# Moving the attention output projection into the first round of experts, with fewer buffers behind it

## The chip, the cores and the metric

The kernel runs on the eight cores of one Trainium2 chip. Each core computes one of the eight sequences of the batch by itself, with its own copy of all weights; no core sends anything to another. The metric is device time: the microseconds of the slowest core for one execution. In the text TensorE is PE in the profile's rows, VectorE is DVE, ScalarE is ACT, GpSimd is POOL, and SyncE is SP. PEld is TensorE's load of the stationary operand.

## The reference, cut to what matters

The layer is a parallel block: the layer norm of x feeds an attention and a mixture of 32 experts, and both are added to x. Per core x is 2048 tokens of 2048 features.

```python
xn = layernorm(x)
# attention, 32 heads of 64, "stick-breaking" weights
z   = q @ k.T / 8 ;  lom = where(mask, -softplus(z), 0)
att = where(mask, exp(log_sigmoid(z) + reverse_cumsum(lom) - lom), 0)
attn = concat_heads(att @ v) @ Wo.T
# experts: all low rank (R = 128), inner width I = 1408
rg, ru = xn @ Rg.T, xn @ Ru.T
for e in range(32):
    g  = silu(rg @ Ug[e].T @ Cg[e].T) ;  u = ru @ Uu[e].T @ Cu[e].T
    y += w[:, e, None] * ((g * u) @ Rd.T @ Ud[e].T @ Cd[e].T)
# one shared expert of the same form with inner width 2816, weight 1
out = x + attn + y + shared
```

w is the top-4 softmax gate, with zeros for the experts that are not chosen. The kernel computes every expert for every token, as the reference does.

## The kernel before, in words

A small recorder (class Sched, L41 to L159) puts each instruction on its engine's list in the order in which the Python code calls it, and works out the semaphore waits from named resources. Each engine executes its own list strictly in that order. Three properties of the recorder matter here:

- A DMA that writes a resource waits for the last writer of that resource, and a whole tile is one resource. So several DMAs that fill parts of one tile run one after the other, each after the landing of the one before.
- A wait for a DMA means a wait for the count that its slot (its semaphore) has reached at the time of recording, and so for every DMA recorded on that slot up to then.
- A read or a write of a part of a tile counts as one of the whole tile.

The stages are: layer norm and gates; attention, head pair by head pair, into the tile oF (64 KB in each partition); the output projection (L715 to L745); and the experts (L749 to L957). In passing, during attention, GpSimd casts the weights of the experts and Wo into scratch tensors in DRAM (scr_cgu, scr_cd, scr_u3, scr_wo).

The projection has four feature blocks ft of 512 columns and 16 token blocks tc. For each ft, 16 DMAs of 128 KB fill one of two wo tiles. For each tc, TensorE adds up 16 matmuls (the weights of Wo against oF) in bank 0 or 1, SyncE loads the piece of x (xp), VectorE adds the two (L740), and SyncE stores the sum.

The experts run over four token blocks tt of 512 tokens. Within a tt, two lanes take turns on all engines. Lane 0 takes the even experts and then the shared one and owns PSUM banks 0 to 3; lane 1 takes the odd experts and owns banks 4 to 7. A turn of a lane is one piece of a generator, here called a slot. An expert (L789) has 15 slots: one with the loads for expert e+2, one head (three matmuls and three copies in a row, L799 to L813), eleven steps over c, one tail (L834 to L844), and one empty one in which the generator ends. A step over c is: two matmuls into banks b1 and b2 (L816, L819), SiLU on ScalarE (L822), the matmul of the previous c by Rd (L826), and a product on VectorE (L830). The shared expert (L847) has 25 slots, 22 of them steps. One turn of both lanes is called a round.

After its units each tt has two sweeps ("half", L916). A sweep holds 256 tokens in eight PSUM banks, and adds up 33 steps of eight matmuls, one step for each expert (L932) and one for the shared expert (L939). The Cd tile of an expert (512 KB) is loaded from DRAM for each sweep, into one of three cd buffers, two steps ahead. At the end VectorE copies four banks into yst0 and four into yst1, and for each an accumulating DMA (L954, slot yacc) adds them to the output in DRAM.

Of the kernel before, what the change touches and what calls it, by code (L numbers as in the profile page):

```python
# [204 lines left out]
def build_program(upto="full", taps=()):  # L205
# [504 lines left out]
    s3 = ExitStack()  # L710
    t_wo2 = [sb(f"wo{i}", [128, NHC * QT], BF16, s3) for i in range(2)]
    t_xp = [sb(f"xp{i}", [128, QT], F32, s3) for i in range(2)]
    t_outp = [sb(f"op{i}", [128, QT], F32, s3) for i in range(3)]
# [1 line left out]
    for ft in range(4):  # L715
        wsl = ft % 2
        t_wo = t_wo2[wsl]
        rwo = res(f"wo{wsl}")
        for hc in range(NHC):
            Sc.dma("POOL", f"lwo{wsl}", lambda s, hc=hc, ft=ft, t_wo=t_wo: s.dma_start(  # L720
                t_wo[:, hc * QT:(hc + 1) * QT],
                d_wo[hc * 128:(hc + 1) * 128, ft * QT:(ft + 1) * QT]),
                reads=[res(f"scr_wo{hc}")], writes=[rwo])
        for tc in range(16):
            bk = tc % 2
            for hc in range(NHC):
                Sc.op("PE", lambda t, hc=hc, tc=tc, ft=ft, bk=bk, t_wo=t_wo: t.matmul(  # L727
                    pbank[bk][:, 0:QT],
                    t_oF[:, hc * S + tc * 128: hc * S + tc * 128 + 128],
                    t_wo[:, hc * QT:(hc + 1) * QT],  # L730
                    start=(hc == 0), stop=True, skip_group_check=(hc != 0)),
                    reads=[roF, rwo], writes=[pr[bk]])
            xs = tc % 2
            rxp = res(f"xp{xs}")
            Sc.dma("SP", f"lxp{xs}", lambda s, tc=tc, ft=ft, xs=xs: s.dma_start(
                t_xp[xs][:], dx[tc * 128:(tc + 1) * 128, ft * QT:(ft + 1) * QT]),
                writes=[rxp])
            osl = tc % 3
            rop = res(f"op{osl}")
            Sc.op("DVE", lambda v, bk=bk, xs=xs, osl=osl: v.tensor_tensor(  # L740
                t_outp[osl][:], pbank[bk][:, 0:QT], t_xp[xs][:], op=ALU.add),
                reads=[pr[bk], rxp], writes=[rop])
            Sc.dma("SP", "sout", lambda s, tc=tc, ft=ft, osl=osl: s.dma_start(
                dout[tc * 128:(tc + 1) * 128, ft * QT:(ft + 1) * QT], t_outp[osl][:]),
                reads=[rop], writes=[OUT_rb[tc]])  # L745
    close_scope(s3)
    close_scope(s_oF)

    s4 = ExitStack()  # L749
    t_rdT = sb("rdT", [128, NIC * 128], BF16, s4)  # L750
    t_su3 = sb("su3", [128, 3 * R], BF16, s4)
    t_scg = sb("scg", [128, SI], BF16, s4)
    t_scu = sb("scu", [128, SI], BF16, s4)
    t_srd = sb("srd", [128, NSC * 128], BF16, s4)
    t_scd = sb("scd", [128, H], BF16, s4)
# [3 lines left out]
    ldc(t_scg[:], dr["sCgT"], "scg", slot="lsh")
    ldc(t_scu[:], dr["sCuT"], "scu", slot="lsh")  # L760
    for c in range(NSC):
        ldc(t_srd[:, c * 128:(c + 1) * 128], dr["sRdT"][c * 128:(c + 1) * 128, :], "srd", slot="lsh")
    ldc(t_scd[:], dr["sCdT"], "scd", slot="lsh")

    t_cgu = [sb(f"cgu{i}", [128, 2 * I], BF16, s4) for i in range(4)]
    t_u3 = [sb(f"u3_{i}", [128, 3 * R], BF16, s4) for i in range(4)]
    t_cd = [sb(f"cd{i}", [128, H], BF16, s4) for i in range(3)]
    t_zg = [sb(f"zg{i}", [128, QT], BF16, s4) for i in range(2)]
    t_zu = [sb(f"zu{i}", [128, QT], BF16, s4) for i in range(2)]
    t_g = [sb(f"g{i}", [128, NIC * QT], BF16, s4) for i in range(2)]  # L770
    t_gu = [sb(f"gu{i}", [128, NIC * QT], BF16, s4) for i in range(2)]
    t_wb = [sb(f"wb{i}", [128, QT], BF16, s4) for i in range(2)]
    t_rds = [sb(f"rds{i}", [128, QT], BF16, s4) for i in range(2)]
    t_zd = sb("zd", [128, (E + 1) * QT], BF16, s4)
    t_werow = [sb(f"werow{i}", [1, QT], BF16, s4) for i in range(4)]
    t_yst = [sb(f"yst{i}", [128, H], F32, s4) for i in range(2)]
# [120 lines left out]
    for tt in range(NTT):  # L897
        for e0 in range(4):
            emit_eloads(e0, tt)
        units = [gen_expert(e, tt, e % 2) for e in range(E)]  # L900
        units.append(gen_shared(tt, 0))
# [76 lines left out]
```

How the kernel before makes its waits and increments, by code:

```python
                def body(e, ops=ops):  # L151
                    for waits, fn, inc_key, inc_n in ops:
                        for (s, v) in waits:
                            e.wait_ge(handles[s], v)
                        if fn is not None:
                            inst = fn(e)
                            if inc_n:
                                inst.then_inc(handles[inc_key], inc_n)
```

## Time and profile before

| | value |
|---|---|
| median of 3 runs | 8514.58 us (8486.89 to 8533.01) |
| profiled execution, its own time | 8456.38 us |
| span of its slowest core (core 2), first to last instruction | 8454.8 us |
| spans of the eight cores | 8384.8 to 8454.8 us |
| TensorE busy, and its weight loads | 5396.6 us (64%), 1591.9 us (19%) |
| VectorE, ScalarE, GpSimd busy | 39%, 34%, 10% |
| granted TensorE clock, mean of core 2 | 0.705 |
| attention ends, projection ends, last sweep ends (core 2) | 4922, 5302, 8428 us |

Busy shares are means over stages that have different limits, so they are read by stage. The granted clock is a share of full speed. A busy TensorE in the profile is not TensorE at its peak, since the recorded durations of matmuls overlap: a 512-column matmul lasts 379 ns in the rows and the next can start 216 ns after it at full clock.

### The profile page before, as it was taken

The numbers are of one execution on the slowest core, as the hardware profiler recorded it, in microseconds if no ns is written. First come the engines' busy times: TensorE is split into PE (matmuls) and PEld (weight loads), VectorE is DVE, ScalarE is ACT, GpSimd is POOL, SyncE is SP. The second block draws the span as 40 slices with busy tenths as digits, with TensorE's granted clock in tenths as the row PEclk, the third lists the DMA queues.
The fourth block names the chain that finished last, engine by engine and source line by source line (L and its number), as shares of the span: only waits on it lengthen the run. The fifth ranks groups of instructions, "written<-read, shape, count | busy, mean of one in ns | idle before, by whom it ended". The sixth has DMA issues, their size and how long they took to land.

```text
span 8454.8 us, 81234 instructions; the slowest of 8 cores (8384.8 to 8454.8 us)
## 1 busy us (share of the span) xinstructions
PE 5396.6 (64%) x17259; PEld 1591.9 (19%) x17588; DVE 3256.7 (39%) x5812; ACT 2889.1 (34%) x4306; POOL 854.1 (10%) x1617
## 2 busy tenths in 40 slices
PE   2222556677766777777677657377667757767776
PEld 0011111122211222221122112112211221122212
DVE  7211224344444444444444411266156425514650
ACT  0000234344444444444444510145044314413440
POOL 0001111110001111000110000100100010011001
PEclk9866655666655666665566579688878887787768
...
GB/s 76 12 5 10 61 52 89 67 12 6 6 6 7 8 8 7 6 6 6 7 8 1 1 68 119 67 55 47 152 82 55 78 148 55 55 122 105 52 35 171
DMA packets 222122, 408.82 MB, mean 48 GB/s; under 512 B 141576, under 2 KB 144032, under 8 KB 215760
## 3 DMA queue, kind: packets, MB, share of 16 engines
...
q10 hardware_dynamic: 272, 0.14, 0.0%
...
## 4 chain that ended last, share of the span: by engine, by line
PE 47%; DMA 16%; DVE 13%; ACT 11%; issue 11%; DVEq 1%; ACTq 0%; SPq 0%; POOL 0%; POOLq 0%; another core or an unknown queue 0%
PE pbq L511 7%; PE zp L646 6%; PE zp L640 5%; DMA cd<-scr_cd 5%; ACT att L566 5%; PE pboA L580 4%; PE zp L549 4%; DVE gu L830 3%; DVE lsb L652 3%; DMA xp<-x 3%; PE pboB L580 3%; ACT g L822 2%; PE pbL L819 2%; DMA wv<-WvT 2%; PE zp L819 2%
## 5 line engine op out<-in xcount | busy, mean ns | idle before, releaser
L652 DVE TENSOR_TENSOR lsb<-zp,z 1x512 bf16<-1x512 f32 (+3 forms) x1152 | 668.3, 588 | 1324.5 <-PE zp L646 1308.7
L580 PE MATMUL pboA<-att,vtok 128*64 128x512 bf16 (+2 forms) x640 | 346.9, 542 | 885.5 <-ACT att L566 738.0
L607 ACT ACTIVATE texp<-zp 128x1024 bf16<-128x1024 f32 x448 | 458.8, 1024 | 912.4 <-PE zp L549 737.3
L566 ACT ACTIVATE att<-zp 128x1024 bf16<-128x1024 f32 x448 | 458.4, 1023 | 679.3 <-DVE lsb L652 439.9
L646 PE MATMUL zp<-lsb,ones 1*128 1x512 bf16 (+2 forms) x1152 | 611.2, 531 | 33.4 <-issue 31.2
L640 PE MATMUL zp<-sp,tri 128*128 128x512 bf16 (+3 forms) x1199 | 596.3, 504 | 55.6 <-DVE z L627 49.0
L627 DVE COPY z<-zp 1x512 f32<-1x512 f32 (+3 forms) x1152 | 623.8, 577 | 0.6 <-issue 0.2
L830 DVE TENSOR_TENSOR gu<-g,pbL 128x512 bf16<-128x512 bf16 x704 | 484.3, 688 | 200.2 <-PE pboB L816 79.1
L830 DVE TENSOR_TENSOR gu<-g,zp 128x512 bf16<-128x512 bf16 x704 | 484.3, 688 | 177.3 <-PE zp L816 56.6
L802 ACT ACTIVATE zg<-zp 128x512 bf16<-128x512 f32 x64 | 38.2, 597 | 1413.8 <-PE zp L799 1413.8
L822 ACT ACTIVATE g<-zp 128x512 bf16<-128x512 f32 x704 | 420.5, 597 | 289.9 <-PE zp L816 221.8
L822 ACT ACTIVATE g<-pboB 128x512 bf16<-128x512 f32 x704 | 420.5, 597 | 243.5 <-PE pboB L816 172.6
L610 ACT ACTIVATE sp<-texp 128x1024 bf16<-128x1024 bf16 x448 | 473.1, 1056 | 42.8 <-ACT texp L607 2.3
L932 PE MATMUL zp<-cd,zd 128*128 128x512 bf16 x1004 | 312.1, 402 | 227.6 <-DMA cd<-scr_cd 221.9
L549 PE MATMUL zp<-q,k 64*128 64x512 bf16 (+3 forms) x1280 | 433.1, 509 | 0.0
L580 PE MATMUL pboB<-att,vtok 128*64 128x512 bf16 (+2 forms) x640 | 359.1, 561 | 0.0
L498 POOL DMA_DIRECT2D wq<-WqT x256 | 135.2, 528 | 2122.1 <-PE zp L556 1090.9
L615 ACT ACTIVATE texp<-zp 128x128 bf16<-128x128 f32 (+2 forms) x384 | 146.7, 382 | 589.0 <-PE zp L556 571.4
L819 PE MATMUL zp<-zu,cgu 128*128 128x512 bf16 x691 | 298.4, 432 | 62.6 <-DVE gu L830 54.8
L819 PE MATMUL pbL<-zu,cgu 128*128 128x512 bf16 x688 | 302.8, 440 | 54.4 <-DVE gu L830 47.3
L727 PE MATMUL zp<-wo,oF 128*128 128x512 bf16 x1003 | 237.3, 389 | 141.6 <-DVE op L740 91.5
L511 PE MATMUL pbq<-xnF,wv 128*128 128x512 bf16 x1008 | 240.4, 390 | 126.6 <-DMA wv<-WvT 119.7
...
## 6 DMA issues: line engine op xcount, KB each, us to landing
cd<-scr_cd POOLq DMA_DIRECT2D x256, 512.0 KB, 4.8
cgu<-scr_cgu POOLq DMA_DIRECT2D x136, 704.0 KB, 4.5
...
```

The lines of the kernel that those rows point to most:

```text
L511: Sc.op("PE", lambda t, hc=hc, nt=nt, bk=bk, wsrc=wsrc: t.matmul(pbank[bk][:, 0:QT], wsrc[:, hc * 128:(hc + 1) * 128], t_xnF[:, hc * S + n ...
L549: Sc.op("PE", lambda t, jb=jb, qt=qt, p0=p0, zp=zp, h0=h0, c0=c0: t.matmul(zpair_ap[zp][:, h0 + c0:h0 + QT], t_k[p0:p0 + 64, jb * 128:(jb ...
L566: Sc.op("ACT", lambda sc, zp=zp: sc.activation(t_att[zp][:], zpair_ap[zp][:], AF.Exp), reads=[pr[(0 if zp == 0 else 6)], pr[(0 if zp == 0 ...
L580: Sc.op("PE", lambda t, zp=zp, pjb=pjb, p0=p0, oc0=oc0, first=first, po=po, hs=hs: t.matmul(pbank[po][0:64, oc0:QT], t_vtok[:, pjb * 128 + ...
L610: Sc.op("ACT", lambda sc, zp=zp: sc.activation(t_sp[zp][:], t_texp[zp][:], AF.Ln, bias=1.0), reads=[res(f"texp{zp}")], writes=[res(f"sp{zp ...
L627: Sc.op("DVE", lambda v, zp=zp, h0=h0, c0=c0, hs=hs: v.tensor_copy(t_z0[hs][:, c0:QT], zpair_ap[zp][0:1, h0 + c0:h0 + QT]), reads=[pr[(0 i ...
L640: Sc.op("PE", lambda t, zp=zp, h0=h0, c0=c0, pz=pz: t.matmul(zpair_ap[zp][:, h0 + c0:h0 + QT], t_tri[:], t_sp[zp][:, h0 + c0:h0 + QT], sta ...
L646: Sc.op("PE", lambda t, zp=zp, h0=h0, c0=c0, pz=pz, hs=hs: t.matmul(zpair_ap[zp][:, h0 + c0:h0 + QT], t_ones1[:], t_lsb[hs][:, c0:QT], sta ...
L652: Sc.op("DVE", lambda v, zp=zp, h0=h0, c0=c0, hs=hs: v.tensor_tensor(t_lsb[hs][:, c0:QT], zpair_ap[zp][0:1, h0 + c0:h0 + QT], t_z0[hs][:, ...
L819: Sc.op("PE", lambda t, c=c, cur=cur, zu=zu: t.matmul(pbank[b2][:, 0:QT], t_cgu[cur][:, I + c * 128: I + (c + 1) * 128], zu[:], start=True ...
L822: Sc.op("ACT", lambda sc, c=c, g=g: sc.activation(g[:, c * QT:(c + 1) * QT], pbank[b1][:, 0:QT], AF.Silu), reads=[pr[b1]], writes=[rg_])
L830: Sc.op("DVE", lambda v, c=c, g=g, gu=gu: v.tensor_tensor(gu[:, c * QT:(c + 1) * QT], g[:, c * QT:(c + 1) * QT], pbank[b2][:, 0:QT], op=AL ...
```

## The change

The projection becomes a generator (gen_attnout) that yields once after the 16 loads of each wo tile and once after each token block tc. A loop drives it together with lane 0 of the first token block: after each piece of the projection, lane 0 gets two slots. The projection now uses banks 6 and 7. When it ends, the remaining units of lane 0 and all odd experts (lane 1) run in the two-lane loop as before, and then the sweeps. The token blocks tt 1 to 3 run as before.

To have the memory for this while oF is still held, tiles are allocated from the other side of SBUF, and four things get smaller: wo has one tile instead of two; cd has two buffers instead of three, loaded one step ahead; yst has one tile instead of two; and expert loads ahead of a token block are for two experts instead of four (in the old code experts 2 and 3 were loaded twice). The rdT tile and the first expert loads are issued ahead of the first wo tile. The tiles of the shared expert and the second lane's tiles are allocated, and loaded, after the projection.

```diff
+    t_wo2 = [sbr("wo0", [128, NHC * QT], BF16)] * 2
+    t_rdT = sbr("rdT", [128, NIC * 128], BF16)
+    t_zg = [sbr("zg0", [128, QT], BF16), None]
...
     for c in range(NIC):
         ldc(t_rdT[:, c * 128:(c + 1) * 128], dr["RdT"][c * 128:(c + 1) * 128, :], "rdT", slot="lrdT")
...
+    def gen_attnout():
+        for ft in range(4):
+            wsl = 0
+            t_wo = t_wo2[0]
+            rwo = res("wo0")
+            for hc in range(NHC):
+                Sc.dma("POOL", f"lwo{wsl}", lambda s, hc=hc, ft=ft, t_wo=t_wo: s.dma_start(
...
+            yield
+            for tc in range(16):
+                bk = 6 + tc % 2
...
+                yield
...
-            for e in range(E + 1):
-                cur = e % 3
+                cur = e % 2
-                if e + 2 < E:
-                    nc_ = (e + 2) % 3
+                if 0 < e + 1 < E and e + 1 >= 2:
+                    nc_ = (e + 1) % 2
...
-                ys = res(f"yst{tci}")
+                ys = res("yst0")
...
+    emit_eloads(0, 0)
+    emit_eloads(1, 0)
+    g_ao = gen_attnout()
+    lane0_q = [gen_expert(e, 0, 0) for e in range(0, E, 2)]
+    cur0 = None
+    while g_ao is not None:
+        try:
+            next(g_ao)
+        except StopIteration:
+            g_ao = None
+            break
+        for _ in range(2):
+            if cur0 is None and lane0_q:
+                cur0 = lane0_q.pop(0)
+            if cur0 is not None:
+                try:
+                    next(cur0)
+                except StopIteration:
+                    cur0 = None
+    close_scope(s_oF)
...
+    ldc(t_su3[:], dr["sU3T"], "su3", slot="lsh")
...
+    t_yst[0] = sb("yst0", [128, H], F32, s4)
+    t_yst[1] = t_yst[0]
+    rest0 = ([cur0] if cur0 is not None else []) + lane0_q
+    rest0.append(gen_shared(0, 0))
+    lane1_q = [gen_expert(e, 0, 1) for e in range(1, E, 2)]
+    drive_units(rest0, lane1_q)
+    y_sweeps(0)
```

TensorE's list between attention and the experts, before. All the projection stands in one piece; zp0 is the tile of banks 0 and 1, and the units of both lanes follow at once:

```order
L580 MATMUL pboB<-att0,vtok1 64x512
L727 MATMUL zp0<-wo0,oF 128x512 x256
L727 MATMUL zp0<-wo1,oF 128x512 x256
L727 MATMUL zp0<-wo0,oF 128x512 x256
L727 MATMUL zp0<-wo1,oF 128x512 x256
L799 MATMUL zp0<-rg,u3_0 128x512
```

The same place after the change, near the projection's end. L752 is a token block's 16 matmuls (zp1 is banks 6 and 7), L810, L813 and L820 are a step over c, L828 and L834 the tail, L793 to L803 the head:

```order
L752 MATMUL zp1<-wo0,oF 128x512 x16
L810 MATMUL zp0<-zg0,cgu0 128x512
L813 MATMUL pbL<-zu0,cgu0 128x512
L820 MATMUL pboA<-gu0,rdT 128x512
L828 MATMUL pboA<-gu0,rdT 128x512
L834 MATMUL zp0<-rds0,u3_0 128x512
L752 MATMUL zp1<-wo0,oF 128x512 x16
L793 MATMUL zp0<-rg,u3_2 128x512
L798 MATMUL zp0<-ru,u3_2 128x512
L803 MATMUL zp0<-werow2,ones1 128x512
L810 MATMUL zp0<-zg0,cgu2 128x512
L813 MATMUL pbL<-zu0,cgu2 128x512
```

Between two pieces of 16 matmuls there now stand two slots of lane 0. By the end of the projection lane 0 is through with nine experts (0 to 16), while lane 1 has not begun.

GpSimd's list (its DMA issues) from the end of attention on, before:

```order
L720 DMA wo0<-scr_wo 128x512 x16
L720 DMA wo1<-scr_wo 128x512 x16
L720 DMA wo0<-scr_wo 128x512 x16
L720 DMA wo1<-scr_wo 128x512 x16
L264 DMA rdT<-RdT 128x128 x11
L264 DMA su3<-sU3T 128x384
L264 DMA scg<-sCgT 128x2816
L264 DMA scu<-sCuT 128x2816
L264 DMA srd<-sRdT 128x128 x22
L264 DMA scd<-sCdT 128x2048
L781 DMA cgu0<-scr_cgu 128x2816
L783 DMA u3_0<-scr_u3 128x384
```

And after the change, first the start and then the place where the projection ends (cgu and u3 are an expert's weights):

```order
L264 DMA rdT<-RdT 128x128 x11
L775 DMA cgu0<-scr_cgu 128x2816
L777 DMA u3_0<-scr_u3 128x384
L775 DMA cgu1<-scr_cgu 128x2816
L777 DMA u3_1<-scr_u3 128x384
L744 DMA wo0<-scr_wo 128x512 x16
```

```order
L264 DMA su3<-sU3T 128x384
L264 DMA scg<-sCgT 128x2816
L264 DMA scu<-sCuT 128x2816
L264 DMA srd<-sRdT 128x128 x22
L264 DMA scd<-sCdT 128x2048
L775 DMA cgu3<-scr_cgu 128x2816
L777 DMA u3_3<-scr_u3 128x384
```

The rdT loads now stand ahead of the first wo tile, all four wo tiles are wo0, and the weights of expert 3 (cgu3, u3_3) stand behind the 26 loads for the shared expert.

TensorE's list late in the first token block, before, in the last steps of the experts 30 (lane 0, zg0) and 31 (lane 1, zg1):

```order
L816 MATMUL zp0<-zg0,cgu2 128x512
L819 MATMUL pbL<-zu0,cgu2 128x512
L826 MATMUL pboA<-gu0,rdT 128x512
L816 MATMUL pboB<-zg1,cgu3 128x512
L819 MATMUL zp1<-zu1,cgu3 128x512
L826 MATMUL zp1<-gu1,rdT 128x512
```

The same part of the list after the change, where expert 29 ends and expert 31 begins:

```order
L820 MATMUL zp1<-gu1,rdT 128x512
L828 MATMUL zp1<-gu1,rdT 128x512
L834 MATMUL pbq<-rds1,u3_1 128x512
L793 MATMUL pbq<-rg,u3_3 128x512
L798 MATMUL pbq<-ru,u3_3 128x512
L803 MATMUL pbq<-werow3,ones1 128x512
L810 MATMUL pboB<-zg1,cgu3 128x512
L813 MATMUL zp1<-zu1,cgu3 128x512
```

Lane 1 stands alone in the list from the end of the shared expert to the first sweep.

## Rows read from the trace of the kernel before

**Rows 1.** Stretches, core 2: start:end, length, busy us (count) per engine, clock, DMA share, GB/s.

```profile
4921.98:4970.28 48.30, 0.00 (x0) 0.14 (x2) 0.60 (x1) 0.00 (x0) 9.12 (x17) 0.50 0.16 52
4970.28:5301.60 331.32, 237.27 (x1003) 97.91 (x1022) 42.86 (x63) 0.00 (x0) 25.21 (x47) 0.97 0.41 118
5301.60:5415.26 113.66, 0.00 (x0) 0.03 (x1) 1.38 (x2) 0.00 (x0) 23.78 (x45) 0.50 0.25 45
5415.26:5913.73 498.47, 358.91 (x1161) 99.42 (x1185) 302.10 (x447) 249.35 (x417) 33.48 (x63) 0.83 0.17 58
5913.73:5960.92 47.19, 31.45 (x69) 5.47 (x69) 17.21 (x25) 14.22 (x24) 0.00 (x0) 0.57 0.00 1
6663.56:6705.36 41.80, 23.52 (x69) 5.21 (x69) 17.19 (x25) 14.22 (x24) 0.00 (x0) 0.92 0.00 1
```

**Rows 2.** Timeline, start of the projection: start, us, engine, line, [idle before <-releaser].

```profile
4925.62 0.54 POOL L720 DMA_DIRECT2D wo<-scr_wo  x1 [3.10 <-DMA wo<-scr_wo]
...
4970.28 15.96 PE L727 MATMUL zp<-wo,oF 128*128 128x512 bf16 x62 [48.85 <-DMA wo<-scr_wo]
```

**Rows 3.** Timeline within the projection.

```profile
4987.13 3.61 PE L727 MATMUL zp<-wo,oF 128*128 128x512 bf16 x16 [0.89 <-DVE op L740]
4987.45 0.43 SPq L735 DMA_DIRECT2D xp<-x  x1
...
4992.49 0.43 SPq L735 DMA_DIRECT2D xp<-x  x1
```

**Rows 4.** Timeline from the projection's end to the first experts.

```profile
5309.44 0.53 POOL L264 DMA_DIRECT2D rdT<-RdT  x1 [118.04 <-DMA out<-op]
...
5338.42 0.54 POOL L264 DMA_DIRECT2D su<-sU3T  x1
...
5408.51 0.55 POOL L781 DMA_DIRECT2D cgu<-scr_cgu  x1
...
5415.26 0.58 PE L799 MATMUL zp<-rg,u 128*128 128x512 bf16 x1 [114.93 <-DMA u<-scr_u]
...
5418.62 0.61 PE L799 MATMUL pbq<-rg,u 128*128 128x512 bf16 x1
```

**Rows 5.** Timeline, shared expert alone: a step at full clock, one at half.

```profile
6700.27 0.69 DVE L880 TENSOR_TENSOR gu<-g,pbL 128x512 bf16<-128x512 bf16 x1 [0.93 <-PE pboA L876]
6701.05 0.60 ACT L872 ACTIVATE g<-zp 128x512 bf16<-128x512 f32 x1 [1.02 <-DVE gu L880]
...
6701.89 0.69 DVE L880 TENSOR_TENSOR gu<-g,pbL 128x512 bf16<-128x512 bf16 x1 [0.93 <-PE pboA L876]
...
5921.22 0.69 DVE L880 TENSOR_TENSOR gu<-g,pbL 128x512 bf16<-128x512 bf16 x1 [1.27 <-PE pboA L876]
...
5923.18 0.69 DVE L880 TENSOR_TENSOR gu<-g,pbL 128x512 bf16<-128x512 bf16 x1 [1.26 <-PE pboA L876]
```

**Rows 6.** Stretches: the first of the eight sweeps, and the sum of all eight.

```profile
5960.92:6044.50 83.58, 63.73 (x259) 24.73 (x264) 1.38 (x2) 0.00 (x0) 15.29 (x29) 0.96 0.60 183
...
sum 654.52, PE 517.70 PEld 198.31 DVE 3.50 ACT 0.00 POOL 122.42; mean PE 64.71 PEld 24.79 DVE 0.44 ACT 0.00 POOL 15.30
```

**Rows 7.** Chain of waits within the first sweep: start, us, what.

```profile
5990.90 4.80 DMA cd<-scr_cd
...
5998.27 4.89 DMA cd<-scr_cd
```

**Rows 8.** Timeline: the same bank in two sweep steps that nothing holds up.

```profile
6138.26 0.38 PE L932 MATMUL pbL<-cd,zd 128*128 128x512 bf16 x1
...
6139.99 0.38 PE L932 MATMUL pbL<-cd,zd 128*128 128x512 bf16 x1
```

**Rows 9.** The cd tile: from issue to landing, over all its loads.

```profile
DMA to landing us min/median/max: 3.6/4.8/12.5
```

**Rows 10.** Timeline: TensorE's first matmul of the second sweep, tt 0 and tt 1.

```profile
6061.34 1.01 PE L932 MATMUL zp<-cd,zd 128*128 128x512 bf16 x2 [17.00 <-DMA cd<-scr_cd]
...
6809.57 1.01 PE L932 MATMUL zp<-cd,zd 128*128 128x512 bf16 x2 [24.04 <-DMA cd<-scr_cd]
```

More of the change, by code:

```diff
@@ L708, in build_program @@
         return nc
[L710 to L713, printed above, removed]
-    roF = res("oF")
[L715 to L755, printed above, removed]
+    def sbr(name, shape, dtype):
+        t = nc.alloc_sbuf_tensor(name, shape, dtype, side="right")
+        sbufs[name] = t
+        r = res(name)
+        r.readers = list(fence)
+        return t
@@ new lines, in build_program @@
+    t_wo2 = [sbr("wo0", [128, NHC * QT], BF16)] * 2
+    t_xp = [sbr(f"xp{i}", [128, QT], F32) for i in range(2)]
+    t_outp = [sbr(f"op{i}", [128, QT], F32) for i in range(3)]
+    t_rdT = sbr("rdT", [128, NIC * 128], BF16)
+    t_cgu = [sbr(f"cgu{i}", [128, 2 * I], BF16) for i in range(4)]
+    t_u3 = [sbr(f"u3_{i}", [128, 3 * R], BF16) for i in range(4)]
+    t_werow = [sbr(f"werow{i}", [1, QT], BF16) for i in range(4)]
+    t_zd = sbr("zd", [128, (E + 1) * QT], BF16)
+    t_zg = [sbr("zg0", [128, QT], BF16), None]
@@ L756, in build_program @@
+    t_zu = [sbr("zu0", [128, QT], BF16), None]
+    t_g = [sbr("g0", [128, NIC * QT], BF16), None]
+    t_gu = [sbr("gu0", [128, NIC * QT], BF16), None]
+    t_wb = [sbr("wb0", [128, QT], BF16), None]
+    t_rds = [sbr("rds0", [128, QT], BF16), None]
+    t_cd = [None, None]
+    t_yst = [None, None]
+    rzd = res("zd")
+    roF = res("oF")
     for c in range(NIC):
         ldc(t_rdT[:, c * 128:(c + 1) * 128], dr["RdT"][c * 128:(c + 1) * 128, :], "rdT", slot="lrdT")
-    ldc(t_su3[:], dr["sU3T"], "su3", slot="lsh")
@@ L759, in build_program @@
[L759 to L776, printed above, removed]
@@ L895, in gen_shared, with drive_units @@
         yield
[L897 to L901, printed above, removed]
+    def drive_units(uq0, uq1):
         lanes = [None, None]
-        qidx = 0
-        uq = [[u for i, u in enumerate(units) if i % 2 == 0],
-              [u for i, u in enumerate(units) if i % 2 == 1]]
+        uq = [list(uq0), list(uq1)]
         while any(uq) or any(l is not None for l in lanes):
@@ L914, in build_program, with y_sweeps @@
                         lanes[p] = None
+    def y_sweeps(tt):
         for half in range(2):
@@ L957, in build_program @@
                     reads=[ys], writes=[OUT_rb[rb]])
+    emit_eloads(0, 0)
[18 more added lines that the diff above has]
+    close_scope(s_oF)
+    s4 = ExitStack()
+    t_su3 = sb("su3", [128, 3 * R], BF16, s4)
+    t_scg = sb("scg", [128, SI], BF16, s4)
+    t_scu = sb("scu", [128, SI], BF16, s4)
+    t_srd = sb("srd", [128, NSC * 128], BF16, s4)
+    t_scd = sb("scd", [128, H], BF16, s4)
+    ldc(t_su3[:], dr["sU3T"], "su3", slot="lsh")
+    ldc(t_scg[:], dr["sCgT"], "scg", slot="lsh")
+    ldc(t_scu[:], dr["sCuT"], "scu", slot="lsh")
+    for c in range(NSC):
+        ldc(t_srd[:, c * 128:(c + 1) * 128], dr["sRdT"][c * 128:(c + 1) * 128, :], "srd", slot="lsh")
+    ldc(t_scd[:], dr["sCdT"], "scd", slot="lsh")
+    for i in range(2):
+        t_cd[i] = sb(f"cd{i}", [128, H], BF16, s4)
+    t_zg[1] = sb("zg1", [128, QT], BF16, s4)
+    t_zu[1] = sb("zu1", [128, QT], BF16, s4)
+    t_g[1] = sb("g1", [128, NIC * QT], BF16, s4)
+    t_gu[1] = sb("gu1", [128, NIC * QT], BF16, s4)
+    t_wb[1] = sb("wb1", [128, QT], BF16, s4)
+    t_rds[1] = sb("rds1", [128, QT], BF16, s4)
+    t_yst[0] = sb("yst0", [128, H], F32, s4)
[5 more added lines that the diff above has]
+    y_sweeps(0)
+    for tt in range(1, NTT):
+        emit_eloads(0, tt)
+        emit_eloads(1, tt)
+        u0 = [gen_expert(e, tt, 0) for e in range(0, E, 2)] + [gen_shared(tt, 0)]
+        u1 = [gen_expert(e, tt, 1) for e in range(1, E, 2)]
+        drive_units(u0, u1)
+        y_sweeps(tt)
     close_scope(s4)
```

26 lines of the change are left out of this document (24 added, 2 removed).

## The prediction

> **What bounds the kernel now.** I went from the stage table to the waits. The stretches of core 2 around the change [rows 1] show five pieces from the end of attention at 4922 us to the first sweep at 5961 us: 48.3 us with TensorE idle, 331.3 us of projection, 113.7 us idle again, 498.5 us of paired experts (240 rounds, so 2.077 us each), and 47.2 us in which the shared expert runs alone. Together that is 1039 us. Attention, before 4922, is not touched.
>
> In the projection TensorE is not the limit. A token block takes 5.04 us from one xp load to the next [rows 3], 5.18 on average (331.3 / 64), while its 16 matmuls take 3.45 (the 3.61 us row ends with one full duration of 0.38, so 15 starts lie 0.215 apart). The store of the sum waits for VectorE's addition, and the next xp load stands behind that store on SyncE's list. So there are some 1.6 us of free TensorE time in each block, 100 in all.
>
> The idle pieces are chains of DMAs. The first is 16 loads of one wo tile, each issued after the last has landed, 3.1 us apart, and TensorE waits 48.9 for them [rows 2]. The second is 11 rdT loads (5309.4 to 5338.4, 29.0 us), then the loads for the shared expert until 5408.5 (70.1 us), then 6.8 us until the first expert's matmul [rows 4].
>
> Of the experts the telling row is the shared expert alone: a step takes 1.62 us at full clock and 1.96 at half [rows 5], since product, SiLU and product must follow each other. A round of both lanes takes 2.077. So a lone lane costs nearly as much time as two.
>
> The sweeps take 654.5 us for eight [rows 6], 81.8 each, or 2.48 for each of 33 steps. A step that nothing holds up takes 1.73 [rows 8]. The chain of waits shows why it is longer: a cd load starts, lands after 4.8, is read, and the load that reuses its buffer starts 7.37 us after the first [rows 7]. With three buffers that is three steps. Of the 7.37 the step itself is 1.73, the landing 4.8 (also the median of all cd loads [rows 9]) and 0.87 lies around them.
>
> **The change part by part**, against the profiled execution's own 8456.4 us.
>
> 1. Start. The rdT chain (29.0) and four more issues of 0.5 now stand ahead of the wo chain, and the expert loads share the engines with its first links: +33. TensorE's idle time grows to about 81. Bounds: +29 (the chain alone) and +40 (the four loads must land first, 6.8 [rows 4] over the 33).
>
> 2. The merged stage. Each block has its 3.45 and then two slots of lane 0. For two steps over c I count, from the end of the 16 matmuls: VectorE first has the addition, until 0.85; the product of c also needs its matmul and SiLU (0.4 + 0.60 and the handovers), so it runs from 1.15 to 1.84; the next step's second matmul waits for it, and one more follows, until 2.35. The second product hides behind the next 16 matmuls. That is 2.35 against 3.24 for two lone steps [rows 5] and 1.3 for six bare matmuls. A head costs 3.4 (5415.26 to 5418.62) [rows 4], a tail 1.3. One expert: 5.5 x 2.35 + 3.4 + 1.3 = 17.6. The 68 pieces of the projection give 136 slots, nine experts of 15. Sum: 64 x 3.45 + 9 x 17.6 = 379, and 12 for blocks with little lane work, where the xp chain still sets 5.04: 391. That is at full clock. The projection alone had a granted clock of 0.97, the pairs 0.83 [rows 1]; at 0.83 the three quarters of it that are TensorE's would add 55. The merged stage is as dense as the pairs, so I take 44: 435. Less 3 for expert 0's head, which hides in the start, and less 331: +101. Bounds: 331 (all lane work free, +0) and 563 (nothing hidden, nine lone experts of 25.8, +232).
>
> 3. One wo tile. At the three changes of ft the chain of 16 can only start when the last block has been read: 48.3 + 0.7 for the issue, less about 4.7 for the four slots that TensorE has in its list before it needs wo: 44 each, +132. Before, the second tile hid this chain. Bounds: 0 (if the loads ran side by side) and 147.
>
> 4. The second gap. The same 26 loads for the shared expert start when the projection has ended, but TensorE now has lane work. Expert 3's weights stand behind them: 0.7 + 70.1 + 6.8 = 77.6 after the projection. TensorE comes to expert 3 after 16 rounds, 33 us, and stands 44, as its list is in order. 113.7 becomes 44: -70. Bounds: -114 and -36.
>
> 5. Remaining units. Lane 0 still has 14 + 6 x 15 + 25 = 129 slots, lane 1 has 16 x 15 = 240. So 129 rounds are paired, 268 us, and 111 slots (7.4 experts) of lane 1 are alone. The lone shared expert took 41.8 at clock 0.92 and 47.2 at 0.57 [rows 1]; less 11 of its 22 steps, an expert alone takes 24.0 to 25.6, so 24.8 x 7.4 = 184. In all 452 for 545.7: -94. This is the small size of the prize: nine experts leave the pairs, but their partners stay. Bounds: -104 and -80.
>
> 6. Two cd buffers. The period of 4.8 + 0.87 + 1.73 now spans two steps, not three. A load also has less company. For its landing I take 4.3, between the fastest (3.6) and the median 4.8 [rows 9]. A sweep is three free steps and 15 periods: 5.2 + 15 x (4.3 + 0.87 + 1.73) = 108.7, times 8 is 870 for 654.5: +215. Bounds: +131 at 3.6, +275 at 4.8. Here the Trainium skill (DMA: Bandwidth & Descriptors, Anatomy of one DMA) puts a load at about 2.0 us plus its bytes by 436 GB/s, an estimate of 3.2 us for 512 KB. By that the term would be +83; no landing in this trace is that short, so the term goes by the rows.
>
> 7. One yst tile. It looks like a new wait in each sweep, but the second yst already waits: both accumulating DMAs share the slot yacc. Only the very first sweep escaped it: TensorE then came back after 17.0 us, against 24.0 after a later one [rows 10]. So +7, once. Bounds 0 and +9.
>
> 8. Fewer loads ahead of a token block and of a sweep: -6 (0 to -20). They come out from behind the same accumulating DMAs.
>
> Sum: 33 + 101 + 132 - 70 - 94 + 215 + 7 - 6 = +318, so 8774 by the profile's own time. The median of the runs shown lies 58 above that execution, so I forecast 8514.6 + 318 = 8833.
>
> **The rivals.**
>
> A. The cd loads land about as fast as the fastest, 3.6: for it speaks that no more than two are in flight; against it that the eight cores read at once and the median with three is 4.8. Term 6 is +131: 8749. The Trainium skill's 3.2 us would make it 8701.
>
> B. The clock falls in the sweeps. TensorE would work 1.73 of each 3.45 us, where it now works 1.73 of 2.48. If it fell to 1.2 GHz, a step would last 3.46: 8 x (10.4 + 15 x (4.3 + 0.87 + 3.46)) = 1119, term 6 is +464, the total 9082. Against it: the shared expert alone, with its waits in every step, had 0.92 in one token block; for it: 0.57 in another [rows 1]. The Trainium skill (TensorE: Matmul & The Clock Gate, HAM oscillation) says that waits for DMAs between short bursts of matmuls bring the low clock back each time; the sweeps' 0.96 [rows 6] with waits of about 0.7 us in most steps don't show it yet.
>
> C. The lane rides free: the merged stage stays bound by the xp chain at 331, as the 100 us of free TensorE time suggest. Against it: nine experts alone have 9 x 37 matmuls, 72 us, but also the handovers. Term 2 is -3: 8729.
>
> D. The merged stage hides nothing, because lane 0's products queue behind additions that wait for xp. 563 instead of 435: 8961.
>
> E. Not slower. One mechanism could do it: transfers land so much faster with fewer in flight that two cd buffers beat three. All else stands at +103. The sweeps must then lose 103, which takes a landing of 1.65 us: 8 x (5.2 + 15 x (1.65 + 2.6)) = 552. At 1.5 it gives 8497. From 1.65 us it decides, and the fastest of 256 loads took 3.6. That nothing else reaches zero is part of the forecast: even with terms 2 and 3 at nothing the sum is +85.
>
> **How the numbers follow.** Forecast 0.60, its own range 8755 to 8915 (terms 2 and 6 each by some 50, the rest by 20, the median by 15). A 0.14, B 0.07, C 0.08, D 0.06, E 0.05. The range 8720 to 8960 takes in A, C and D nearly whole and leaves out B, E and thin tails. About 0.5%, 43 us, is what a measurement of this kernel can tell from no change. Only E is not slower: faster 0.03, same 0.02, slower 0.95.
>
> **What would show it.** Right: TensorE idle for about 80 us after attention; three idle pieces of about 44 inside the merged stage, each ended by a wo load; blocks of 6 to 7 us between them; one idle piece of about 44 some 33 us after the last projection matmul, ended by a u3 load; then lone steps of 1.6 to 2.0 us for about 184; sweeps of 105 to 115 us, with cd waits in every second step; no new wait for yst but in the first. Wrong: sweeps near 82 us, or merged blocks near 5.2 or above 8. The total would be wrong by most if the sweeps were, as they are two thirds of the sum.

## The result, and the profile after

The changed kernel takes 8816.46 us (median of 10 runs, 8779.24 to 8899.12) where the kernel before took 8523.94 in the runs beside it: a ratio of 1.0382, 95% interval 1.0335 to 1.0428 (the comparison of runs leaves disturbed ones out, so it is not the ratio of the two medians). The forecast of 8833 was a ratio of 1.037. The profiled execution took 8849.9 us, with a span of 8848.4 on core 7.

Core 7 ran at a granted clock of 0.691 and core 2 at 0.703. The rows of before are of core 2 at 0.705, so core 2 makes the fairer comparison: its span went from 8454.8 to 8768.7 us, +313.9. I show the stretches of both. They are attention's end to the projection's first matmul, the merged stage, the rest of tt 0's experts in which both lanes work, the part in which one lane is alone, and the first sweep. The columns are those of [rows 1].

```profile
core 7: us, PE busy (x) PEld busy (x) DVE busy (x) ACT busy (x) POOL busy (x), PEclk, DMA share, GB/s
4915.97:5000.84 84.87, 1.75 (x3) 0.33 (x4) 1.30 (x2) 1.19 (x2) 17.57 (x33) 0.50 0.20 53
5000.84:5578.55 577.71, 377.52 (x1354) 141.09 (x1355) 129.26 (x188) 69.94 (x116) 35.36 (x66) 0.76 0.25 83
5578.55:5899.59 321.04, 213.27 (x644) 57.34 (x643) 163.93 (x240) 134.75 (x226) 28.73 (x54) 0.70 0.18 46
5899.59:6112.20 212.61, 137.50 (x280) 22.88 (x279) 73.71 (x107) 57.91 (x97) 7.45 (x14) 0.51 0.09 29
...
6112.19:6214.75 102.56, 62.23 (x259) 23.53 (x260) 0.00 (x1) 0.00 (x0) 15.84 (x30) 0.98 0.50 154
...
sum 864.48, PE 530.00 PEld 196.94 DVE 0.01 ACT 0.00 POOL 126.67; mean PE 66.25 PEld 24.62 DVE 0.00 ACT 0.00 POOL 15.83
```

The same stretches of core 2:

```profile
4916.75:4997.12 80.37, 1.17 (x2) 0.34 (x4) 1.30 (x2) 1.19 (x2) 17.57 (x33) 0.50 0.20 56
4997.12:5535.17 538.05, 330.38 (x1328) 131.92 (x1355) 129.30 (x188) 70.00 (x116) 35.36 (x66) 0.85 0.28 89
5535.17:5852.06 316.89, 199.66 (x631) 55.80 (x643) 163.12 (x240) 134.74 (x226) 28.72 (x54) 0.76 0.18 47
5852.06:6062.91 210.85, 133.09 (x273) 22.74 (x278) 73.69 (x107) 57.91 (x97) 7.45 (x14) 0.53 0.09 29
```

From attention's end to the first sweep core 2 took 1146.2 us where it took 1038.9 [rows 1]: +107. The eight sweeps, cut in each kernel from the first matmul to the first copy into yst, took 848.6 where they took 650.8: +198. All else made 9. So two thirds of the loss are the sweeps, and none of it is in attention.

The waits of the merged stage stand in the timeline of core 7, TensorE's rows: start, us, form, [idle before, what ended it]. They answer to [rows 2] and [rows 4].

```profile
5000.84 6.30 PE L752 MATMUL zp<-wo,oF 128*128 128x512 bf16 x16 [48.76 <-DMA wo<-scr_wo]
...
5161.89 6.22 PE L752 MATMUL zp<-wo,oF 128*128 128x512 bf16 x16 [42.78 <-DMA wo<-scr_wo]
...
5310.81 3.55 PE L752 MATMUL zp<-wo,oF 128*128 128x512 bf16 x9 [42.11 <-DMA wo<-scr_wo]
...
5469.12 1.44 PE L752 MATMUL zp<-wo,oF 128*128 128x512 bf16 x3 [40.14 <-DMA wo<-scr_wo]
...
5655.83 0.58 PE L793 MATMUL pbq<-rg,u 128*128 128x512 bf16 x1 [40.23 <-DMA u<-scr_u]
```

Three new holes of 40 to 43 us, each ended by a load of the one wo tile, and a fourth where the lane needs its next u3. Between them the blocks look like this; they answer to [rows 3], where a block took 5.04.

```profile
5022.94 3.70 PE L752 MATMUL zp<-wo,oF 128*128 128x512 bf16 x16
...
5026.47 0.44 PE L810 MATMUL zp<-zg,cgu 128*128 128x512 bf16 x1
...
5029.24 4.38 PE L752 MATMUL zp<-wo,oF 128*128 128x512 bf16 x16
...
5036.21 4.11 PE L752 MATMUL zp<-wo,oF 128*128 128x512 bf16 x15
```

Starts are 6.30 and 6.97 us apart: the 16 matmuls, then 2.6 to 2.8 us in which two lane steps pass through three engines. The second block is longer for its matmuls: from the first of them to the lane's next one it is 3.53 us, then 4.20. The granted clock of core 7 was 1.00 until 5026 us and 0.81 behind it, and 0.76 over the whole merged stage, where core 2 had 0.85:

```profile
5026.02:5043.87 17.85, 14.02 (x51) 5.04 (x49) 6.18 (x9) 2.98 (x5) 0.54 (x1) 0.81 0.24 76
```

In the sweeps the chain of waits shows the cd loads that answer to [rows 7], the landing over all loads answers to [rows 9], and TensorE's restart in the second sweep of tt 0 and of tt 1 to [rows 10]:

```profile
6138.17 3.78 DMA cd<-scr_cd
...
6144.51 3.89 DMA cd<-scr_cd
...
6150.96 3.80 DMA cd<-scr_cd
```

```profile
DMA to landing us min/median/max: 3.6/3.9/10.1
```

```profile
6239.39 1.01 PE L922 MATMUL zp<-cd,zd 128*128 128x512 bf16 x2 [23.24 <-DMA cd<-scr_cd]
...
7067.49 1.01 PE L922 MATMUL zp<-cd,zd 128*128 128x512 bf16 x2 [24.77 <-DMA cd<-scr_cd]
```

A period is now 6.34 to 6.45 us and spans two steps; before, 7.37 spanned three. The page's group of these matmuls says it in one line, and its section on DMA issues gives the load:

```profile
L922 PE MATMUL zp<-cd,zd 128*128 128x512 bf16 x1024 | 324.1, 404 | 433.5 <-DMA cd<-scr_cd 429.6
...
cd<-scr_cd POOLq DMA_DIRECT2D x256, 512.0 KB, 3.9
```

TensorE stood 433.5 us before matmuls that lasted 324.1.

### The profile page after: what moved, and what is told of

Read it like the earlier page. It is cut to its first block, busy times and chain, and to the rows that moved or that the text cites. A ratio compares the mean times of both kernels' runs of the same rounds, so it can differ in the third digit from the quotient of the medians.

```text
span 8848.4 us, 80371 instructions; the slowest of 8 cores (8737.1 to 8848.4 us)
## 1 busy us (share of the span) xinstructions
PE 5605.0 (63%) x17588; PEld 1615.5 (18%) x17588; DVE 3261.8 (37%) x5812; ACT 2888.2 (33%) x4306; POOL 845.8 (10%) x1601
## 4 chain that ended last, share of the span: by engine, by line
PE 48%; DMA 16%; DVE 12%; ACT 10%; issue 10%; another core or an unknown queue 2%; DVEq 1%; ACTq 0%; POOL 0%; POOLq 0%; SPq 0%
PE pbq L511 7%; DMA cd<-scr_cd 6%; PE zp L640 5%; PE zp L646 5%; ACT att L566 4%; PE pboA L580 3%; DVE gu L824 3%; PE zp L549 3%; PE zp L752 3%; DVE lsb L652 3%; PE pboB L580 2%; PE zp L813 2%; PE pbL L813 2%; ACT g L816 2%; DMA wo<-scr_wo 2%
## 5 line engine op out<-in xcount | busy, mean ns | idle before, releaser
L640 PE MATMUL zp<-sp,tri 128*128 128x512 bf16 (+3 forms) x1280 | 642.5, 508 | 55.6 <-DVE z L627 49.0
L922 PE MATMUL zp<-cd,zd 128*128 128x512 bf16 x1024 | 324.1, 404 | 433.5 <-DMA cd<-scr_cd 429.6
L752 PE MATMUL zp<-wo,oF 128*128 128x512 bf16 x1024 | 282.8, 440 | 173.8 <-DMA wo<-scr_wo 173.8
L813 PE MATMUL zp<-zu,cgu 128*128 128x512 bf16 x704 | 323.7, 460 | 81.0 <-DVE gu L824 75.8
L940 DVE COPY yst<-zp 128x512 f32<-128x512 f32 x32 | 22.1, 692 | 908.1 <-PE zp L929 905.6
L813 PE MATMUL pbL<-zu,cgu 128*128 128x512 bf16 x704 | 315.7, 448 | 60.2 <-DVE gu L824 54.8
```

The costliest lines, as they stand in the source:

```text
L640: Sc.op("PE", lambda t, zp=zp, h0=h0, c0=c0, pz=pz: t.matmul(zpair_ap[zp][:, h0 + c0:h0 + QT], t_tri[:], t_sp[zp][:, h0 + c0:h0 + QT], sta ...
L813: Sc.op("PE", lambda t, c=c, cur=cur, zu=zu: t.matmul(pbank[b2][:, 0:QT], t_cgu[cur][:, I + c * 128: I + (c + 1) * 128], zu[:], start=True ...
```

## The experiments

**e1_cd3** gives the changed kernel its third cd buffer back, in memory that wo no longer needs by then:

```diff
-                cur = e % 2
+                cur = e % 3
-                if 0 < e + 1 < E and e + 1 >= 2:
-                    nc_ = (e + 1) % 2
+                if e + 2 < E:
+                    nc_ = (e + 2) % 3
...
+    for i in range(2, 3):
+        t_cd[i] = t_wo2[0].ap()[:, (i - 2) * H:(i - 1) * H]
```

> The changed kernel with a third cd buffer again (placed in the memory of the wo tile, which is free by then), loaded two steps ahead as before the change. Nothing else differs. My theory: two buffers make the period of 6.5 us (landing, 0.87, one step) span two steps instead of three, and that is two thirds of the loss. Then the sweeps fall from about 108 us to 80 to 84 each, the landing of a cd load rises again from 3.9 to 4.6 to 4.9 us, and the ratio to the kernel before falls from 1.038 to 1.010 to 1.017. Rival: the sweeps are long for another reason (the lower clock after waits, or the single yst tile): then they stay above 100 us and the ratio above 1.03.

Measured: 8589.64 us, ratio 1.0113 [1.0061, 1.0165]. The difference of the ratios, 0.0269, is 229 us, and the sweeps of core 7 fell by 228, from 864.5 to:

```profile
6122.28:6200.60 78.32, 59.90 (x259) 24.22 (x260) 0.00 (x1) 0.00 (x0) 15.30 (x29) 0.98 0.63 195
...
sum 636.91, PE 494.68 PEld 192.11 DVE 0.01 ACT 0.00 POOL 122.42; mean PE 61.83 PEld 24.01 DVE 0.00 ACT 0.00 POOL 15.30
```

Loads land slower again (median 4.8 us) and the sweeps are faster all the same: what counts is how many steps one landing spans.

**e5_before_cd2** makes that one cut in the kernel before: `cur = e % 2`, the load for e + 1 instead of e + 2.

> The kernel before with one edit: two cd buffers, loaded one step ahead. It does that part of the change alone. Theory: the sweeps grow from 81 to about 107 us each, the landing falls from 4.8 to about 3.9 us, the whole takes 200 to 220 us more: ratio 1.022 to 1.028. Rival: in the changed kernel the sweeps are long also because of the merging or the other order of loads: then the ratio is under 1.018.

Measured: 8738.57 us, ratio 1.0309 [1.0254, 1.0365], more than expected. The sweeps alone take 856.2 us on core 6 and 848.6 on core 2, some 200 more than before; the lower end of the interval is 216. A load lands in 3.6, 3.8 and 15.4 us (shortest, median, longest). So the size by rows is that of term 6, and the ratio holds 15 to 60 us more. In the profiled execution the rest lies outside the edit: cores 6 and 7, its slowest, took 388 and 413 us for the projection, where the other six took 319 to 334 us. What slowed those two is not shown.

**e7_before_yst1** (a single run) gives the kernel before a single yst tile: `t_yst = [sb("yst0", ...)] * 2`.

> The kernel before with one yst tile instead of two, nothing else. One look. Theory: the second yst already waits for the accumulating DMA of the first through their shared slot, in every sweep but the very first. So TensorE's idle time after the first sweep grows from 17.0 to about 24 us, and the other seven places stay at 23 to 25; the whole at most 10 us more. Rival: a single tile adds a wait of about 8 us to each of the eight sweeps: the other places grow to 31 to 33, 60 us in all.

Measured: 8453.9 us. TensorE comes back for the second sweep of tt 0 after 23.85 us instead of 17.00 [rows 10], later after 23.55 to 23.78, as before:

```profile
6086.81 1.01 PE L932 MATMUL zp<-cd,zd 128*128 128x512 bf16 x2 [23.85 <-DMA cd<-scr_cd]
...
6835.53 1.01 PE L932 MATMUL zp<-cd,zd 128*128 128x512 bf16 x2 [23.55 <-DMA cd<-scr_cd]
```

The tile costs one wait of 7 us, as term 7 says.

**e2_noslots** is the changed kernel without the merging: `for _ in range(0):` for `range(2)`, so that the projection runs alone and lane 0's experts follow.

> The changed kernel with no slot of lane 0 inside the projection: all units run after it, in pairs, with all the other edits in place. This undoes the merging alone. My theory: merging is worth next to nothing, as a lone lane costs as much as a pair. From the end of attention to the first sweep I expect 85 + 331 + 3 x 48 + about 46 (expert loads behind the shared expert's) + 498 + 47 = 1151 us, against about 1146 to 1196 for the changed kernel (cores 2 and 7): ratio to before 1.030 to 1.043. Rival: the nine experts that ran in the projection's free TensorE time are a real gain, hidden by the other edits. Then this kernel loses the nine experts' share, 100 us and more: ratio 1.050 or above.

Measured: 8815.71 us, ratio 1.0395 [1.0342, 1.0448]; after has 1.0382. From attention's end to the first sweep it takes 1114.2 us on core 5 and 1108 to 1125 on all cores, where after takes 1138 to 1151 on cores 0 to 5 and 1191 and 1197 on the other two. The wo waits are then 84.3, 49.8, 50.3 and 49.4, longer than merged. The stretches are the projection, and all experts:

```profile
5033.93:5477.54 443.61, 238.81 (x1025) 99.23 (x1025) 42.88 (x62) 0.00 (x0) 25.74 (x48) 0.82 0.30 88
5477.54:6063.81 586.27, 388.34 (x1255) 104.29 (x1253) 320.45 (x474) 263.59 (x441) 46.70 (x88) 0.80 0.18 51
```

The rival, that the merging itself recovers a good part of what the buffers cost, is refuted: as built, it moves time about and gains none that can be measured. By the stage it even costs some 20 to 30 us, which the ratios don't show.

**e4_balanced** asks why. In the projection lane 0 takes experts 0, 1, 2, ... in order; what is left goes to both lanes in turn, the shared expert to lane 1:

```diff
-    lane0_q = [gen_expert(e, 0, 0) for e in range(0, E, 2)]
+    lane0_q = []
+    nxt_e = 0
...
+                cur0 = gen_expert(nxt_e, 0, 0)
+                nxt_e += 1
...
-    rest0 = ([cur0] if cur0 is not None else []) + lane0_q
-    rest0.append(gen_shared(0, 0))
-    lane1_q = [gen_expert(e, 0, 1) for e in range(1, E, 2)]
+    rest0 = ([cur0] if cur0 is not None else []) + [gen_expert(e, 0, 0) for e in range(nxt_e + 1, E, 2)]
+    lane1_q = [gen_expert(e, 0, 1) for e in range(nxt_e, E, 2)]
+    lane1_q.append(gen_shared(0, 1))
```

> The changed kernel with the experts taken in their natural order during the projection (0 to 8 on lane 0), and the remaining 23 experts and the shared one dealt out to both lanes evenly. So 179 rounds are paired and 11 slots alone, instead of 129 and 111. The work within the projection is the same. My theory: lane 1 alone is why nine hidden experts bring so little; the units after the projection fall from 452 us by the forecast (268 + 184) to about 392, 60 us less, ratio to before 1.029 to 1.034. The stall for the weights behind the shared expert's loads changes little. Rival: lone rounds are as cheap as half a pair by now: less than 15 us, ratio 1.036 or more.

Measured: 8742.18 us, ratio 1.0275 [1.0241, 1.0308]. From the projection's end to the first sweep (core 6):

```profile
5588.90:6037.73 448.83, 293.06 (x921) 79.72 (x920) 236.79 (x347) 192.71 (x323) 36.15 (x68) 0.76 0.17 46
```

448.8 us for 527.7 (core 2) and 533.7 (core 7) in after. The lane that runs alone cost about 80 us, more than the 60 expected.

**e3_parwo** gives each of the 16 parts of a wo tile a dependency record of its own (`rh = res(f"wo0_{hc}")`, written by its load, read by its matmul).

> The changed kernel with a resource of its own for each of the 16 parts of the wo tile, so that the 16 loads of a tile are issued one behind the other without waiting for each other's landing. Same bytes, same tile, same number of loads. My theory: the three pieces of 40 to 43 us within the merged stage and the first wait of 45 to 49 us are the chain of landings; side by side the 16 loads take about 11 us, so each piece falls to under 10 us and the first by about 37: 130 to 150 us less, ratio to before 1.018 to 1.026. Rival: the loads are limited by bandwidth (2 MB, and eight cores at once): then the pieces stay above 25 us and the ratio above 1.030.

Measured: 8799.73 us, ratio 1.035 [1.0313, 1.0387]. The first wo wait fell to 5.64 us, the later ones only to 38.6, 39.8 and 40.1. My expectation missed: the 16 loads still share one semaphore slot, and the wait of a part is for the latest count of that slot. This run doesn't settle term 3.

**e3b_parwo16** adds a semaphore slot per part:

```diff
-                Sc.dma("POOL", f"lwo{wsl}", lambda s, ...
+                Sc.dma("POOL", f"lwo{wsl}_{hc}", lambda s, ...
```

> As e3_parwo, but each of the 16 parts of the wo tile has also a DMA slot of its own. In e3_parwo only the first tile came side by side (wait 5.6 us); for the later ones the writer of each part was the shared slot at its latest count, so each load still waited for the one before and the waits stayed at 38.6 to 40.1 us. That left the question open. Theory: chain of landings. Now the three later waits fall to under 10 us, some 100 us less than e3_parwo: ratio to before 1.018 to 1.026. Rival: bandwidth, or that TensorE is late anyway: waits above 25 us, ratio 1.030 or more.

Measured: 8668.92 us, ratio 1.0197 [1.0156, 1.0237]. Core 1, the merged stage, and the first block at the first change of ft, which starts without any idle time where after had 40 to 43 us:

```profile
4978.02:5417.97 439.95, 361.83 (x1356) 137.63 (x1355) 129.90 (x189) 70.09 (x116) 39.41 (x75) 0.86 0.37 112
```

```profile
5088.29 3.62 PE L755 MATMUL zp<-wo,oF 128*128 128x512 bf16 x16
```

No wo wait is above 4 us. Against after the ratio is 0.0185 lower, 157 us: the three waits (125) and the start (on core 1 37 us, where it was 80) make 168, and the merged stage gave a little back on cores 0 to 3 (438 to 461 us, where after has 409 to 416 without its waits). So the one tile isn't what costs, the chain of 16 loads is, and that answers terms 1 and 3.

**e6_before_par** gives each part of the wo tiles, of rdT and of srd a record of its own in the kernel before. The semaphore slots stay shared, as in e3_parwo, so of the four wo tiles only the first two come side by side:

> The kernel before with the loads of the first wo tiles, of rdT and of srd issued side by side (a resource for each part), nothing else changed: the idle pieces around the projection attacked without merging. Theory: the 48 us ahead of the projection become about 10, the 114 us behind it about 45 (the store, 11 + 4 + 22 issues of 0.53 us, the experts' loads): 105 us less, ratio 0.985 to 0.990. Rival: the many small casting loads are limited by something else than the wait for each other: ratio 0.995 or more.

Measured: 8350.2 us, ratio 0.9818 [0.9784, 0.9851]. The first gap fell from 48.85 [rows 2] to 12.22 us, the second from 113.66 [rows 1] to 37.39 (core 3):

```profile
5000.13 10.09 PE L730 MATMUL zp<-wo,oF 128*128 128x512 bf16 x39 [12.22 <-DMA wo<-scr_wo]
...
5360.61 0.58 PE L810 MATMUL zp<-rg,u 128*128 128x512 bf16 x1 [37.39 <-DMA u<-scr_u]
```

Of the 162.5 us in these two gaps, 112.9 were not a lack of work for TensorE but loads that waited for each other. The ratio is below the range expected: it stands for 155 us, and where the 42 beyond the two gaps come from is not shown.

**e8_best** puts it together: e3b_parwo16, e4_balanced, rdT and srd side by side, and five cd buffers (three in wo's memory), four loads ahead.

> All repairs together on the changed kernel: parts of wo, rdT and srd side by side, the remaining experts dealt out to both lanes evenly, and five cd buffers, three of them in the memory of the wo tile, loaded four steps ahead. If the terms add up: 1.038 less 0.026 for cd at three buffers, 0.010 for balance, about 0.025 for the chains (213 us) and up to 0.016 for sweeps that run at 65 to 70 us instead of 82, as now bandwidth or TensorE would set them: ratio 0.960 to 0.975. Rival: more loads in flight only land later, since the sweeps are limited by bandwidth: sweeps stay at 78 to 82, ratio 0.975 to 0.985.

Measured: 8083.52 us, ratio 0.9512 [0.9483, 0.954]. This is faster than both kernels. Core 3's first two sweeps, and all eight:

```profile
5824.92:5883.73 58.81, 58.10 (x259) 25.58 (x260) 0.00 (x0) 0.00 (x0) 14.24 (x27) 0.96 0.72 242
5910.38:5969.01 58.63, 58.07 (x259) 25.71 (x260) 0.01 (x1) 0.00 (x0) 14.25 (x27) 0.96 0.83 274
...
sum 468.67, PE 464.89 PEld 205.24 DVE 0.01 ACT 0.00 POOL 113.98; mean PE 58.11 PEld 25.65 DVE 0.00 ACT 0.00 POOL 14.25
```

TensorE is busy for 464.9 of 468.7 us, and a step is 58.6 / 33 = 1.78 us, close to the free step of 1.73 [rows 8]. The rival that the memory would give out is refuted: core 3 drew 242 and 274 GB/s in these two sweeps while the other seven ran the same kernel, where three buffers drew 183 [rows 6] and two 154. My expectation was too cautious.

**e9_best_noslots** and **e10_best_1slot** vary the merging in that kernel: `range(0)` and `range(1)` for `range(2)`.

> e8_best with no slot inside the projection: the same repairs (loads side by side, five cd buffers, experts dealt out evenly), but all units after the projection. It asks what merging is worth once the lanes are balanced. Theory: nine experts cost the projection about 120 us (the changed kernel, core 7: 577.7 less 125.0 of wo waits less 331) and save half a pair each, 9 x 15.6 = 140, so merging is worth 0 to 50 us: ratio 0.951 to 0.958. Rival: the merged stage hides more than that once nothing stalls it: ratio 0.962 or more.

> e8_best with one slot of lane 0 for each piece of the projection instead of two, so four and a half experts are hidden and not nine. Theory: the first slot of a block rides mostly in the 1.6 us that TensorE is free under the xp chain, the second one is mostly paid for. So the merged stage falls from about 450 us (without waits) to 345 to 370, and the 4.5 experts moved back cost 70 us: the same as e8_best or up to 30 us better, ratio 0.947 to 0.953. Rival: both slots cost the same: the same ratio as the mean of e8_best and e9_best_noslots.

Measured: 8186.05 us, 0.9614 [0.9548, 0.9681], and 8217.77 us, 0.9646 [0.9578, 0.9714]. With nothing else in its way the merging is worth 0.0102 by the ratios, 87 us, a value between the theory's range and the rival's. By the stage from attention's end to the first sweep (867 to 898 us on the eight cores without, 848 to 878 with) it is about 30. Which of the two is right is open. One slot is no better than none, which neither theory expected. Its stage took 942 to 976 us on cores 0, 1, 4 and 5, and 886 to 909 on the other four, so the runs show no single size for it. The merged part is shorter, the rest longer (core 4):

```profile
4982.28:5362.01 379.73, 286.19 (x1190) 117.05 (x1190) 80.10 (x123) 36.51 (x60) 30.19 (x58) 0.92 0.44 117
5362.01:5914.88 552.87, 367.31 (x1088) 98.62 (x1088) 280.32 (x413) 227.22 (x381) 43.06 (x81) 0.80 0.18 49
```

In that rest a pair of experts takes 35.1 us, in e8_best 32.4, in e9_best_noslots 31.8. The lanes start their experts half an expert apart here, as the projection ended in the middle of one.

**e11_1slot_phase** tests this: the half-done expert is finished alone, and then both lanes start together.

```diff
+    if cur0 is not None:
+        for _ in cur0:
+            pass
```

> As e10_best_1slot, but the expert that lane 0 has half done at the projection's end is finished alone, and only then both lanes start, each with a fresh expert. In e10 the heads of the two lanes lie half an expert apart, and a pair takes 35.1 us (5400.2 to 5821.7 us, 12 pairs, core 4), against 32.4 in e8_best and 31.8 in e9. Theory: it is this offset that ate the gain of the single slot; in phase a pair takes 31.5 to 32.5 again, so attention's end to the first sweep takes 860 to 885 us instead of 950 to 965: ratio to before 0.948 to 0.957. Rival: the pairs are slow for another reason (single slot, load order), they stay above 34.5 us, ratio 0.962 or more.

Measured: 8179.97 us, ratio 0.9575 [0.946, 0.969]. Twelve pairs took 31.5 us each on core 0, as expected if the offset costs; on all cores it is 31.1 to 32.0, where e10 has 34.6 to 35.7. The stage took 828 to 862 us on seven cores and 920 on core 0, on most cores less than in e8_best. But the ratio, from three runs, has so wide an interval that e11 is told apart neither from e8_best nor from e9 and e10.

## Why the prediction was right, and where it was not

Term by term, in us against the kernel before; the columns are what the terms of the sum said and what two cores of the changed kernel show, both against core 2 of the kernel before.

| Term | Predicted | Core 2 | Core 7 |
|---|---|---|---|
| 1 start | +33 | +32 | +37 |
| 2 merged stage without wo waits | +101 | +82 | +121 |
| 3 three wo waits | +132 | +125 | +125 |
| 4 second gap | -70 | -73 | -73 |
| 5 remaining units | -94 | -58 | -52 |
| 6 sweeps | +215 | +198 | +214 |
| 7 yst, once | +7 | +6 | +6 |

**1, 3 and 4** came as chains of loads counted link by link. Right, and e3b_parwo16 and e6_before_par show the mechanism: when the chain goes, so does the wait. The waits at the changes of ft were 40 to 43, not 44, since a lane slot more stood ahead.

**2.** 538.05 less the 125.1 of its waits on core 2 leaves 412.9; on core 7 452.7. The predicted 435 lies between, and the two differ in the granted clock, 0.85 and 0.76. That it lies between is in part luck. By its own terms the cost of a clock of 0.83 is 60 us (293 us of TensorE's share by 1 / 0.83 - 1), not 55, and the 44 taken in its place was a choice that no row fixes. Rival C (the lane rides free) would need 331, rival D 563: both refuted.

**5 is the step that failed.** "An expert alone takes 24.0 to 25.6": it takes 28.3. The bounds of -104 and -80 didn't hold it. The rows of core 7 show a lone expert's last products, and the next one's first (VectorE's rows), with TensorE's two starts of an expert:

```profile
5999.46 0.59 PE L793 MATMUL pbq<-rg,u 128*128 128x512 bf16 x1 [0.94 <-DVE zd L837]
...
6023.84 0.69 DVE L824 TENSOR_TENSOR gu<-g,zp 128x512 bf16<-128x512 bf16 x1 [1.27 <-PE zp L820]
...
6026.89 0.69 DVE L837 CAST zd<-pbq 128x512 bf16<-128x512 f32 x1 [0.84 <-PE pbq L834]
...
6027.73 0.59 PE L793 MATMUL pbq<-rg,u 128*128 128x512 bf16 x1 [0.95 <-DVE zd L837]
...
6032.56 0.69 DVE L824 TENSOR_TENSOR gu<-g,zp 128x512 bf16<-128x512 bf16 x1 [0.61 <-ACT g L816]
```

From last product to first product is 8.72 us, ten steps of 1.96 [rows 5] are 19.6, together 28.3. I had taken the shared expert alone less 11 of its 22 steps, which left too little for head and tail, and half of it came from a unit at a clock of 0.92; the lone stretch here had 0.51 to 0.53 throughout. 7.4 experts by 28.3 are 209; the stretch on core 2 took 210.9. The paired rounds took 276.7 for 268. That lost 36 to 42 us, and terms 2, 3 and 6 gave it back on core 2 (43 us together); the forecast is better than its parts, and that is luck.

**6.** The size was right, the composition only in part. The landing was 3.9, between the 4.3 of the forecast and the 3.6 of rival A, and the term would then be 8 x (5.2 + 15 x (3.9 + 0.87 + 1.73)) = 822, or +167. The first sweep took just that, 102.56 for 102.7. The other seven took 107.5 to 111.0. An idle gap ahead of a sweep does not tell them apart: four of the seven begin after 23 us or more, the other three straight after the shared expert, like the first. The second sweep of core 7, its stretches in the columns of [rows 1]:

```profile
6239.39:6262.00 22.61, 17.14 (x48) 5.97 (x48) 0.00 (x0) 0.00 (x0) 2.81 (x6) 0.72 0.36 109
6262.00:6290.00 28.00, 15.09 (x64) 5.69 (x64) 0.00 (x0) 0.00 (x0) 4.58 (x9) 1.00 0.55 168
6290.00:6320.00 30.00, 18.38 (x74) 6.94 (x75) 0.00 (x0) 0.00 (x0) 4.75 (x9) 0.95 0.49 151
6320.00:6350.00 30.00, 18.25 (x73) 6.88 (x72) 0.00 (x0) 0.00 (x0) 3.70 (x7) 0.94 0.46 141
```

and in its timeline two matmuls after a cd wait, then two some 3 us later:

```profile
6256.39 0.63 PE L922 MATMUL pbL<-cd,zd 128*128 128x512 bf16 x1
6256.81 0.63 PE L922 MATMUL pboA<-cd,zd 128*128 128x512 bf16 x1
...
6259.63 0.38 PE L922 MATMUL pboA<-cd,zd 128*128 128x512 bf16 x1
6259.85 0.38 PE L922 MATMUL pbq<-cd,zd 128*128 128x512 bf16 x1
```

Starts are 0.42 us apart, then 0.22: the engine ran at 1.2 GHz, then at 2.4. With a granted clock of 0.77 the period from 6248.12 to 6255.58 is 7.46 us, a microsecond more than at full clock. That is rival B in small: a granted clock of 0.72 for the first 22.6 us, 0.94 to 1.00 after. As a whole, with 9082 us, it is refuted. Later in the sweep the clock fell twice for 3.4 us, each time at the end of a wait of about 3 us behind a load that landed late, after 5.4 and 5.2 us. The first of them, from the chain of waits and from TensorE's rows:

```profile
6284.92 5.40 DMA cd<-scr_cd
...
6290.45 1.01 PE L922 MATMUL zp<-cd,zd 128*128 128x512 bf16 x2 [3.22 <-DMA cd<-scr_cd]
```

The Trainium skill (TensorE: Matmul & The Clock Gate, HAM oscillation) describes waits for DMAs between bursts that bring the low clock back each time. The trace agrees in part: the clock fell behind the waits of 2.2 us in the first steps and at the two of about 3 us. Behind waits of 2.71 and 2.74 us (ended at 6263.58 and 6298.12) it stayed at 1.00, and so it did behind most others, 0.8 to 1.8 us long. How much of the 42 us between 822 and 864 comes from the clock and how much from late landings was not measured apart.

**7** is shown by e7_before_yst1. **8** did not come: the idle time ahead of tt 1's experts was 24 to 27 us as before. Rival E would need sweeps below 552 us; they were never near it with two buffers.
